# A two-layer graph kernel: preparation in another order, identity products in early lots, layer two added to the output by accumulating transfers

## The reference

```
h = max(layernorm(x), 0)
x = x + segment_sum(einsum(h, W0[type])[type, src], dst) + b0
h = max(layernorm(x), 0)
deg = segment_sum(1, dst);  dinv = rsqrt(deg + 1)      # a self loop is added
x = x + leaky_relu(dinv * (A @ (dinv * h) + dinv * h) @ W1 + b1, 0.2)
```

## Time and profile before

| | |
|---|---|
| median of 3 runs | 2270.48 us (2268.88 to 2272.52) |
| the profiled execution | 2259.58 us, span 2258.0 us |
| PE, PEld | 1980.5 us (88%), 1785.3 us (79%) |
| DVE, ACT | 1284.2 us (57%), 1608.3 us (71%) |
| POOL | 1617.2 us (72%) |
| granted TensorE clock, mean | 0.948 |

### The profile page before, as it was taken

The page is one execution under the profiler, slowest core; times in us unless marked ns, Lnnn a source line. Parts: engine busy times, 40 slices in busy tenths (PEclk is TensorE's granted clock), DMA queues, the critical chain, the costliest instruction groups (busy, mean ns, idle before and its releaser), DMA issues.

```text
span 2258.0 us, 44551 instructions
## 1 busy us (share of the span) xinstructions
PE 1980.5 (88%) x14179; PEld 1785.3 (79%) x14179; DVE 1284.2 (57%) x3610; ACT 1608.3 (71%) x3919; POOL 1617.2 (72%) x1725
## 2 busy tenths in 40 slices
PE   1467877878989899888999999999999999999998
PEld 1356776877878788777888899998988898889876
DVE  6556656657767766865776652333233234454667
ACT  5636767777878778777887887677767768686631
POOL 2677777777777777777777777777777777777614
PEclk7678998999999999889999999999999999999999
DMA  8535456555665755565675668655556556666645
GB/s 282 161 103 155 147 149 183 163 151 171 194 182 163 222 162 158 165 184 165 212 207 169 185 186 256 193 156 168 162 150 183 151 152 165 156 168 154 144 117 167
DMA packets 378364, 387.34 MB, mean 172 GB/s; under 512 B 243555, under 2 KB 299152, under 8 KB 378000
## 3 DMA queue, kind: packets, MB, share of 16 engines
q0 software_dynamic: 78832, 215.52, 33.2%
q1 hardware_dynamic: 253760, 123.65, 20.1%
q10 hardware_dynamic: 45536, 45.26, 6.0%
HBM read 307.32 MB, written 76.96 MB: 170 GB/s over the span
## 4 chain that ended last, share of the span: by engine, by line
PE 59%; POOL 19%; issue 8%; ACT 7%; DMA 2%; DVE 1%; ACTq 1%; DVEq 0%; POOLq 0%
PE ps_slot L1623 20%; POOL rows_f L1092 18%; PE ps_slot L1685 13%; PE ps_proj L1639 11%; PE ps_aux L1685 9%; PE ps_slot L1653 3%; ACT staged_f L1274 2%; DMA rows_f<-table,idxT 2%; ACT gap_f L1339 2%; PE ps_slot L1704 1%; ACT wide_f L1332 1%; ACT onehot_f L1347 1%; POOL recs_f L1080 1%; ACT acc_f L1260 1%; PE ps_proj L1704 0%
## 5 line engine op out<-in xcount | busy, mean ns | idle before, releaser
L1092 POOL DMA_INDIRECT rows_f<-table,idxT x1612 | 1533.6, 951 | 492.2 <-issue 475.2
L1623 PE MATMUL ps_slot<-onehot_f,rows_f 128*128 128x128 f32 x6448 | 869.1, 287 | 127.8 <-DMA rows_f<-table,idxT 100.9
L1623 PEld LDWEIGHTS ps_slot<-onehot_f,rows_f 128*128 128x128 f32 x6448 | 824.2, 201 | 161.0 <-DMA rows_f<-table,idxT 114.2
L1339 ACT ACTIVATE gap_f<-iota,keyT 128x128 bf16<-128x128 bf16 x1614 | 527.6, 395 | 72.5 <-ACT staged_f L1274 45.6
L1274 ACT ACTIVATE staged_f<-ps_slot 128x400 uint8<-128x400 f32 x800 | 345.3, 500 | 164.2 <-PE ps_slot L1653 162.5
L1519 DVE TENSOR_TENSOR hots_f<-ps_slot,keys_f 128x400 bf16<-128x400 bf16 x800 | 287.2, 359 | 284.2 <-PE ps_slot L1653 279.2
L1639 PE MATMUL ps_proj<-w0t,acc_f 128*128 128x256 f32 x1600 | 372.0, 387 | 0.9 <-DVE xt_f L1437 0.7
L1347 ACT ACTIVATE onehot_f<-gap_f 128x384 f32<-128x384 bf16 x538 | 277.4, 516 | 121.6 <-PE ps_slot L1623 121.2
L1332 ACT ACTIVATE wide_f<-abuf_f 128x512 fp32r<-128x512 uint8 (+1 forms) x488 | 270.0, 611 | 99.8 <-PE ps_slot L1685 70.9
L1639 PEld LDWEIGHTS ps_proj<-w0t,acc_f 128*128 128x128 f32 x1600 | 305.4, 196 | 40.5 <-issue 1.0
L1522 DVE TENSOR_TENSOR hots_f<-ps_slot,keys_f 128x512 bf16<-128x512 bf16 x800 | 332.5, 416 | 0.0
(11 more groups left out here) (162 smaller groups left out, 966.3 us busy)
## 6 DMA issues: line engine op xcount, KB each, us to landing
rows_f<-table,idxT POOLq DMA_INDIRECT x1612
abuf_f<-counts_d SPq DMA_DIRECT2D x70, 320.0 KB
stash_f<-table SPq DMA_DIRECT2D x14, 1280.0 KB, 8.6
table<-hs_f SPq DMA_DIRECT2D x47, 256.0 KB
table<-xres SPq DMA_DIRECT2D x10, 640.0 KB, 4.2
acc_f<-x_d SPq DMA_DIRECT2D x50, 128.0 KB, 2.5
x_d<-xt_f SPq DMA_DIRECT2D x49, 128.0 KB
xt_f<-in_x_dram SPq DMA_DIRECT2D x48, 128.0 KB
```

What stands on the lines that cost most here:

```text
L1092: eng.indirect_dma_start(rows0[:, k, c, :], None, V["table0"], bass.IndirectOffsetOnAxis(ap=idxT[:, n * LOT + c:n * LOT + c + 1], axis=0)) ...
L1339: last = eng.activation(gap[:, n % 2, c, :], iota[:, :], ACT.Abs, scale=-1.0, bias=V["key"][:, n * LOT + c:n * LOT + c + 1])
L1623: last = eng.matmul(o[:, b * W:(b + 1) * W], rows0[:, k, c, b * P:(b + 1) * P], onehot[:, n % HOTS, c, :], start=(c == 0), stop=(c == chun ...
```

## The change

**Preparation.** The rows of the chunk numbers (`chunk_rows`, four small VectorE operations out of `edge_ends`) come first. `edge_offsets` comes ahead of the statistics of batches 4 and 5, `edge_keys` behind them, `copy_starts` ahead of the last two batches. ScalarE takes the next batch's square root behind the third ReLU of a batch; it copies the indices after batch 3, the keys at the end. SyncE writes and reads the small arrays at separate places. The window starts are turned into a bank of their own.

**Identity products.** In slots 16 to 199 that have no piece, none just before, and no projection, TensorE does six 128x128 bf16 products of the identity into ps_aux, whose result nobody reads. There are 97 such slots; the last is 182.

**First unit of the last batch.** TensorE does both halves of its first two tiles (8 products) before it waits for the rows of the last tile, and then the last 4.

**Layer two's sum.** SyncE stores layer one's x1 straight into the output. For 46 of the 50 tiles GpSimd starts a transfer that adds the leaky ReLU's result to the output rows; for the last four SyncE loads the rows back, VectorE adds them (`add_x1`) and SyncE stores them. GpSimd's add is gone, and so are 46 loads and 46 stores by SyncE. The ring of results is NOUT = 8, and the leaky ReLU waits for the transfer eight tiles back.

```diff
-NOUT = 4
+FILL = (16, 200, 6)
+NOUT = 8
+DIRECT = 4
...
@@ SyncE, preparation @@
                 for li, (a, b) in enumerate(XL):
-                    if li == 3:
-                        compare_ends()
+                    if li == 2:
+                        put_ends()
+                    if li == 5:
+                        get_neighbours()
+                    if li == NX - 1:
+                        get_starts()
                     eng.wait_ge(S["h32"], li + 1)
                     eng.dma_start(table0[a * P:b * P, :].rearrange("(t p) d -> p t d", p=P), xres[:, a:b, :]).then_inc(s_t0, 16)
-                    if li == NX - 2:
-                        window_starts()
+                    if li == NX - 3:
+                        put_starts()
...
@@ ScalarE, preparation @@
                     for t in range(a, b):
                         last = eng.activation(xres[:, t, :], xres[:, t, :], ACT.Relu, scale=rs[:, t:t + 1], bias=nb[:, t:t + 1])
+                        if t == a + 2 and li + 1 < NX:
+                            root(li + 1)
                     last.then_inc(S["h32"], 1)
...
-                    if li + 1 < NX:
-                        root(li + 1)
                     if li == 1:
                         cast_edges()
-                    if li == 5:
-                        sum_unsorted()
+                    if li == 3:
+                        for i in range(KT):
+                            copy_keys(i)
                     if li == 4:
                         store_records()
-                    if li == 6:
-                        for i in range(KT):
-                            copy_keys(i)
-                    if li == 7:
-                        for i in range(KT, 2 * KT):
-                            copy_keys(i)
+                        sum_unsorted()
+                for i in range(KT, 2 * KT):
+                    copy_keys(i)
...
@@ VectorE, preparation @@
+                chunk_rows()
                 stats(0)
                 for li in range(1, 4):
                     stats(li)
                     scales(li - 1)
                 edge_ends()
-                stats(4)
-                scales(3)
                 edge_offsets()
+                for li in (4, 5):
+                    stats(li)
+                    scales(li - 1)
                 edge_keys()
-                stats(5)
-                scales(4)
+                stats(6)
+                scales(5)
                 pair_ends()
-                for li in range(6, NX):
+                stats(7)
+                scales(6)
+                copy_starts()
+                for li in range(8, NX):
                     stats(li)
                     scales(li - 1)
                 scales(NX - 1)
-                copy_starts()
...
@@ GpSimd, behind the gathers @@
-            for k in range(T):
-                eng.wait_ge(s_lk, k + 1)
-                eng.wait_ge(s_xi[k % NOUT], 16 * (k // NOUT + 1))
-                if k >= NOUT:
-                    eng.wait_ge(s_o[k % NOUT], 16 * (k // NOUT))
-                eng.tensor_tensor(zz[:, k % NOUT, :], hh[:, k % 4, :], xin[:, k % NOUT, :], ALU.add).then_inc(s_z, 1)
+            def add_to_out(k):
+
+                t = PL.order[k]
+                eng.wait_ge(s_lk, k + 1)
+                for i in range(2):
+                    eng.wait_ge(s_st[i], parts_stored(t)[i])
+                rows_out, a, b = out_rows(t)
+                eng.dma_start(rows_out, hh[a:b, k % NOUT, :], accum_op=ALU.add).then_inc(s_o[k % NOUT], 16)
+
+            for k in range(T - DIRECT):
+                add_to_out(k)
...
@@ SyncE, store of layer one, and the loads and stores at the end @@
-                eng.dma_start(x1_d[t * P:(t + 1) * P, :], x_home(t)).then_inc(s_st[t % 2], 16)
+                rows_out, a, b = out_rows(t)
+                eng.dma_start(rows_out, x_home(t)[a:b, :]).then_inc(s_st[t % 2], 16)
...
-                for k in PL.fin.get(n + 1, ()):
-                    if k >= NOUT:
-                        put_out(k - NOUT)
-                    load_x1(k)
-            for k in range(T - NOUT, T):
+            for k in range(T - DIRECT, T):
+                load_x1(k)
+            for k in range(T - DIRECT, T):
                 put_out(k)
...
@@ VectorE, closing a tile @@
-                if k >= 4:
-                    eng.wait_ge(s_z, k - 3)
-                eng.scalar_tensor_tensor(hh[:, k % 4, :], yy[:, k % 4, :], 0.2, yy[:, k % 4, :], ALU.mult, ALU.max).then_inc(s_lk, 1)
+                if k >= NOUT:
+                    eng.wait_ge(s_o[k % NOUT], 16 * (k // NOUT))
+                eng.scalar_tensor_tensor(hh[:, k % NOUT, :], yy[:, k % 4, :], 0.2, yy[:, k % 4, :], ALU.mult, ALU.max).then_inc(s_lk, 1)
+
+            def add_x1(k):
+
+                i = k - (T - DIRECT)
+                a, b = out_rows(PL.order[k])[1:]
+                eng.wait_ge(s_lk, k + 1)
+                eng.wait_ge(s_xi[i], 16)
+                eng.tensor_tensor(hh[a:b, k % NOUT, :], hh[a:b, k % NOUT, :], xin[a:b, i, :], ALU.add).then_inc(s_z, 1)
...
@@ TensorE @@
+            def dense_first_of_last(u):
...
+                eng.wait_ge(E["lo"], T - 1)
+                for half in range(2):
+                    i = piece_no(u, half)
+                    if PL.before[i] is not None:
+                        eng.wait_ge(s_da, PL.before[i] + 1)
+                steps = [(half, t) for half in range(2) for t in range(m - 1)] + [(0, m - 1), (1, m - 1)]
+                for half, t in steps:
...
+                    if half == 0 and t == m - 1:
+                        eng.wait_ge(E["lo"], T)
...
+            def keep_clock(n):
+
+                done = [piece_no(u, half) for m in range(n) for u, half in PL.pieces.get(m, ())]
+                if done:
+                    eng.wait_ge(s_da, max(done) + 1)
+                for _ in range(FILL[2]):
+                    eng.matmul(ps_aux[:, 0:P], identb[:, :], identb[:, :], start=True, stop=True)
...
+                if FILL[0] <= n < FILL[1] and n not in PL.pieces and n - 1 not in PL.pieces and n not in PL.project:
+                    keep_clock(n)
```

More of the change, by code:

```diff
@@ L941, in both_layers @@
         s_z = sem("z")
-        s_xi = [sem(f"x_in{i}") for i in range(NOUT)]
+        s_xi = [sem(f"x_in{i}") for i in range(DIRECT)]
+        s_out = sem("stored_out")
         s_o = [sem(f"out{i}") for i in range(NOUT)]
@@ L1609, in _ @@
                     close(k)
+                    if k >= T - DIRECT:
+                        add_x1(k)
         @block.tensor
```

78 lines of the change are left out of this document (48 added, 30 removed).

## The result

The kernel before took 2269.17 us (median of 6 runs, 2265.08 to 2272.52), the changed one 2256.33 us (median of 6, 2250.04 to 2256.82). The ratio is 0.9938, with a 95% interval of 0.9923 to 0.9953: 12.8 us at the medians, 14.1 by the ratio. On a second chip it was 0.9939 (0.9923 to 0.9955). The direction was as forecast.

What follows compares the result with a forecast made beforehand. GpSimd's gathers were taken to pace the main stage, TensorE's chain the tail. Preparation 6.6, seam 0.7 and tail 1.1, identity products 0, gave 8.4 us off 2270.48, so 2262.1 us; own range 2259 to 2265, wider range 2256 to 2270.

Steps and rivals of the forecast that it cites:

- What bounds the kernel: Whole run: the first gather's time moves everything; TensorE before 830 us counts only if it holds up a gather.
- Preparation, 6.6 us: Start of the run: checks start at 52.8 instead of 59.38, the first gather at 61.4, saving 6.6 us.
- 1.4 us for handovers: Preparation: allowance added for ScalarE and VectorE handing over to each other, before the checks start at 52.8.
- the upper bound, 9: Preparation: the most it could save, 9 us, if all named idle time of ScalarE comes back.
- the two waits, 3.98 and 4.71: Preparation: ScalarE's idle times before batch 3 (3.98 us, to stay) and before batch 4 (4.71 us, to go).
- the second copy of the ends: Preparation: the small VectorE operation assumed to be blocked beside GpSimd until 27.84.
- Identity products, 0: TensorE up to slot 182: 44 to 87 us of added products, hidden by waits for gathered rows, worth 0.
- Seam, 0.7: First unit of the last batch: starts 0.66 us earlier, taken as 0.7 us saved; 2.1 if the clock stays up.
- The fall of the clock, 1.4 us: Seam: the lower clock behind the wait costs 1.4 us; whether the shorter gap prevents it was left undecided.
- Tail, 1.1: End of the run: cheaper closes by VectorE end at 2250.3 against 2251.47, 1.1 us saved; slots stay 6.25 us.
- Rival A: Tail: adding transfers are dear, from 1.56 us each GpSimd's queue sets the pace; 2273.5 at 1.78; chance 0.12.
- Carrying the saving over from the profiled execution: Sum: 8.4 us, worked out on the profiled 2259.58, taken unchanged off the timed median 2270.48, giving 2262.1.

Runs made afterwards that it cites:

- e2: The kernel before with the preparation's part of the change alone: ratio 0.9956 (0.9942 to 0.9969), 10.0 us off.
- e12: The changed kernel with the next batch's square root behind the fifth ReLU again instead of the third: ratio 0.9953 to the kernel before.
- e6: The kernel before with the 582 identity products alone: ratio 0.9985 (0.9972 to 0.9998).
- e4: The changed kernel without its 582 identity products: ratio 0.9956 (0.9944 to 0.9969) to the kernel before.
- e10: The changed kernel with 202 more identity products near ten TensorE waits, lots 244 to 308, mostly one slot off: ratio 0.9983 to the kernel before.
- e11: The changed kernel with 20 and 10 identity products in front of the seam's two waits: ratio 0.9932 (0.9919 to 0.9946) to the kernel before.
- e1: The kernel before, unchanged, profiled and timed again against itself: ratio 1.0001, profiled 2270.97 us.
- e3: The changed kernel with the old preparation: ratio 0.9978 (0.9969 to 0.9987) to the kernel before, 5.0 us off.
- e5: The changed kernel, unchanged, once more beside the kernel before on another chip: ratio 0.9939 (0.9923 to 0.9955), profiled 2251.35 us.
- e8: The kernel before with the first unit of the last batch reordered alone: ratio 0.9989 (0.9977 to 1.0000).
- e13: e11 with the stash load of slot 233 waiting for lot 234 to be summed, on a slow chip: ratio 0.9977 to the kernel before.
- e17: The same kernel as e13 on the other slow chip: ratio 0.9975 (0.9959 to 0.9991) to the kernel before.
- e9: The changed kernel with the counts of units 18 and 19 loaded sooner, at slot 215: ratio 0.9951 (0.9938 to 0.9964) to the kernel before.

## Why the prediction was right or wrong

- **What bounds the kernel: right.** What moves the first gather moves the run: e2, with only that change, gave 10.0 us (7.0 to 13.1) for a first gather 8.0 to 8.3 us sooner. No gather was held up before 830 us (19 waits for TensorE, none over 0.3 us).
- **Preparation, 6.6 us: the step that failed, a term that was mis-sized (the start of ScalarE's work and the handovers).** The first gather came at 59.06 and not at 61.4, so the saving is 9.0. ScalarE's work was summed well: 19.7 us forecast from the batch 3 ReLU to the last root, 19.5 found (30.61 to 50.15), in which the only idle time, 0.52 us, is already contained. But I started it at 31.3, where it started at 30.61 (0.7 us), and added 1.4 us for handovers on top, of which nothing came on top. So the checks (L414) started at 50.58 and not at 52.8. e12 shows why so little was needed: the root behind the third ReLU gives VectorE its time while ScalarE still has two ReLUs to do; without it the gaps are 0.45 to 0.71 at each batch. I named that effect and then charged an allowance against it. What I gave as the upper bound, 9, was the value, though not for the reason given with it: of the two waits, 3.98 and 4.71, only the second went. This step explains 2.4 of the 4.4 us between the forecast saving and the 12.8 measured. Seam and tail gave 0.3 less than forecast, so 2.3 us more came from somewhere that no term names (below). That VectorE stays blocked beside L334 was right (3.08 us), but it was a tensor_tensor of `edge_offsets` (L367) and not the second copy of the ends; that one (L361, 2.23 us) stood beside GpSimd's casts before it. The Trainium skill's rule of the shared port (SBUF — State Buffer, "Who interferes with whom") agrees with the row of L367.
- **Identity products, 0: not refuted, not shown, on the ordinary chips.** The clock of 130:530 is 0.92 (0.90 before), the gathers there stand at 1.25 us each as before, as forecast. e6 alone (0.9985) and e4 (0.9956 without them, 0.9938 with, on another chip) point to 3 or 4 us of gain, e6 with an interval that reaches nearly to nothing and e4 with intervals that overlap; the hold-up is no smaller in the kernels that have them (0.9, 2.4, 5.7 and 7.7 us) than in those without (1.1 to 9.1), so no way by which they would help is seen. On the slow chips they cost 6 to 13 us.
- **Seam, 0.7: right in size.** From the first projection behind the lots to the first of the tail, 29.81 us (2146.02 to 2175.83) against 30.30. The unit started 0.46 us sooner and not 0.66, since the wait that is left ends with one more add of VectorE (L1576 at 2165.48, 128x256) than the one that I had read as the last. The fall of the clock, 1.4 us, stayed in most executions, as I left open; the 0.90 us of idle time decides nothing by itself, since the clock fell behind it in the changed kernel and not in e10. The products of e11 remove the fall and win 1.5. The Trainium skill (TensorE: Matmul & The Clock Gate, "Part 1: The HAM clock gate") has the clock follow recent activity, and the stretches of e11 agree: with products in the gaps it reads 1.00 where it was 0.69 and 0.50. Why it also read 1.00 in e2 and e10, with the gaps empty, no run here shows.
- **Tail, 1.1: right.** 72.7 against 73.7 us, L1591 at 0.425 us, transfers at 0.925. Rival A needed 1.56 and is out. A slot did not change. To the end of the span the tail is worth 1.25 us, in every execution: 78.8 to 79.1 us from its first projection with adding transfers, 80.1 to 80.4 without (e11's span lacks its last 3.5 us and is left out).
- **Carrying the saving over from the profiled execution: right by luck.** I did not ask why that execution was 10.9 us under the median. By e1 it had been spared up to 5.1 us of hold-up and 4.8 of gather issue. After's profiled execution, with 7.7 us of hold-up, lies at its median. If the median executions of both kernels have a like share of both, which the few profiles make likely and don't show, the difference of the medians was little touched, while the two profiled spans differ by only 3.3 us.

The terms that the traces show, 9.0, 0.5 and 1.0, make 10.5 us; the medians differ by 12.8, with an interval from 10.7 to 17.5 by the ratio. So the traces' sum lies just outside what was measured. e3 says the same from the other side: 5.0 us (2.9 to 7.0) for what the profiles give 1.5. What makes the rest is open. The identity products, which e4 and e6 put at 3 to 4 us without a trace of how, are one candidate. Another is the gathers' own time: 1532.5 to 1535.3 us in the seven profiled executions of kernels with new preparation and new tail on the ordinary chips, 1537.6 to 1538.8 in six of the seven of the others, with both groups on one and the same chip twice (e1 to e4, e5 to e8). Such 4 us would more than fill the rest. But the first of before had 1533.6, and on the slow chips one and the same kernel had 1535.4 and 1538.6 (e13 and e17), so the kernel alone does not set it.

Also open: whether the stash load sets the hold-up. The correlation with TensorE's waits for rows is shown, e9 speaks against the two count loads, and the delay of the stash was tried only on chips where it could not show.

## What to carry to other kernels

Profile the kernel before more than once before taking a sum from it: two executions of this one differ by 11.4 us, nearly as much as the change is worth, and the waits per line, less their usual 0.30 us, say for half of it which of them was fortunate. When two engines hand over to each other, don't charge a lump for handovers; look whether the small operation now stands inside the other engine's work (here two ReLUs long), and if it does, charge nothing. Products that keep the clock up paid here inside a gap in front of dense work on the critical path (1.5 us for 30 products at the seam); 202 of them mostly one slot beside their gaps cost 6 us or more. And before a clock that stayed up in one execution is put down to a change, see in how many executions it stays up without it.

## What the runs showed of the hardware

- An adding transfer of 128 rows of 1 KB takes GpSimd 0.925 us on the mean to issue, less than a gather of the same size with its gap (1.25), lands after 3.4 us at the median, and does not slow VectorE's operation with two SBUF inputs beside it (L1591 at 0.425 us; 0.656 beside GpSimd's adds).
- The issue of a gather differs a little between executions as a whole: 951 to 953 ns on the mean in some, 954 or 955 in others. In the two of before it is 951 and 954, and from 500 us on 2 to 4 ns apart in every stretch of 400 us, 5 us over 1612 gathers.
- Behind the same waits of 1.79 and 0.90 (or 1.35) us at the seam, the granted clock fell to 0.50 in eleven of thirteen executions and stayed at 1.00 in two; with 30 products in those waits it stayed at 1.00 in seven of seven.
- On two chips every version that ran there, before too, took 19% longer, with gathers at 951 to 954 ns as elsewhere and idle time of TensorE that nothing in the profile ends. Which engine bounds a kernel can differ from chip to chip.
